# A gated block on one core: LoRA coefficients transposed two weight pieces later, and GpSimd's work cut into strips

## The chip, the cores and the metric

The kernel runs on one core of a Trainium2 chip. The core has five engines with queues of their own: TensorE (PE in the profile, with its weight loads as PEld), VectorE (DVE), ScalarE (ACT), GpSimd (POOL), and SyncE (SP), which here only starts transfers. Each works through its instructions in the order in which they are written and waits for others by semaphores. The metric is the device time of one execution in microseconds; the median of three executions stands for the kernel.

## What is computed

Two layers over 2048 tokens of width 2048 (the two batches of 1024 lie one after the other). The first multiplies the normalised and quantised tokens with a quantised context matrix of their batch. The second is a dense product with a weight matrix plus a mixture of eight LoRA experts of rank 16, of which a router picks two for each token.

```python
def fake_quant(x, s, z):
    return (jnp.clip(jnp.round(x / s + z), 0, 255) - z) * s

x = x + tanh(g_xattn[0]) * matmul(fake_quant(layernorm(x), s1, z1), fake_quant(ctx, s2, z2))

h = layernorm(x)
base = jnp.einsum('bsd,od->bso', h, base_W)
probs = softmax(jnp.einsum('bsd,ed->bse', h, router_W))
top_vals, top_idx = jax.lax.top_k(probs, 2)
w_dense = (one_hot(top_idx, 8) * (top_vals / top_vals.sum(-1, keepdims=True))[..., None]).sum(-2)
mid = jnp.einsum('bsd,edr->bser', h, lora_A) * w_dense[..., None]
x = x + tanh(g_ffn[0]) * (base + jnp.einsum('bser,erd->bsd', mid, lora_B) * 2.0)
```

## The kernel before, in words

**First stage (0 to some 300 us of the span).** Sixteen tiles of 128 tokens go through statistics and scale on VectorE (`x_stats`, `x_scale`), quantisation on ScalarE (`x_to_u8`), widening to bf16 on either (`x_widen`, tile `a_rows`), a transposition on TensorE (line 1361, tile `aT_psum`) and a copy back. They are multiplied with the context in 64 units of 16 matmuls (line 1374). VectorE empties each unit's bank into the tile of x (`evac`, line 1048). The order of all this is written out by hand in slot tables (`SCALE_SLOT`, `UNIT_SLOT`, `COLADD_SLOT` and others, 558 slots): each engine runs over the slots and does what its tables hold for a slot.

**GpSimd's part.** It has three kinds of work. `row_term` (line 677) adds a number per token to a whole tile of x, 128x2048, 16 times, and must be done before the tile's first `evac`. `add_col_term` (line 685) adds a row to a block of 128x512 after its `evac`, 64 times; the stores of x and the statistics of the second layer wait for it. `t_step` (line 694) subtracts two 128x1024 halves of the weights in f32, 32 times: these are the sums of weight blocks of a Strassen product, in eight jobs of four steps. Jobs 0 and 1 run by the slot tables in the first stage, jobs 2 to 7 in the second. Each step waits for the one before it by a semaphore, the first of a job for its load. A job's result is stored to `w_sums_scratch` by SyncE, and the load of job j from 4 on waits for the store of job j-2, in the same queue that loads the weights.

**Second stage.** The tokens go in four groups of 512. For the first group the plain product is taken: four blocks of 512 output columns (`plain_block`), each over eight weight pieces of 256 rows, 24 matmuls of 128x512 each, and a piece of LoRA B. `at_piece` counts the weight pieces of this group, 0 to 31, and every engine's program is laid out by it. A piece is loaded by SyncE into one of six buffers, its high part is made by ScalarE (`w_hi`, line 802) and its low part by VectorE (`w_lo`, line 1082), three pieces ahead of its product, and each product is three matmuls (lines 1389 to 1391). In f32 the low part is `w_stage` minus `w_hi`, both in SBUF.

While TensorE multiplies pieces 0 to 3, VectorE also works out the router's weights in eight parts (`router`, lines 1140 to 1172), each behind a `w_lo` in its order. The last part writes `mid_scaled`. TensorE transposes it into `col_psum` (`mid_transposes`, line 1447), ScalarE makes its high part (`mth`, line 881) and VectorE its low part (`mid_lo`, line 1182, semaphore `mtl_ready`). The LoRA products that end each block need both. In the kernel before, TensorE transposes right after the products of piece 4, ScalarE copies in its step for piece 5, VectorE in its step for piece 6, and TensorE waits for `mtl_ready` ahead of piece 7's products. The other three groups (the Strassen part, from about 502 us) have transposes of their own, in slot 4.

Of the kernel before, what the change touches and what calls it, by code (L numbers as in the profile page):

```python
# [25 lines left out]
ALU = mybir.AluOpType  # L26
# [107 lines left out]
SLOTS_G = 14  # L134
JOBS = 8
GROUPS = (2, 0, 1, 3)
FILL_AT = (8, 9, 10, 11, 13, 14, 16, 17)
# [129 lines left out]
def build(nc, x, ctx, wt, ar, lb, scal, x1s, wts, out):  # L267
    es = ExitStack()
    with es:
# [392 lines left out]
        def _(pool):  # L662
# [11 lines left out]
            def row_term(t):  # L674
                pool.wait_ge(row_ready, t + 1)
                tile = xg[(t // M) % 2][:, t % M, :]
                pool.tensor_scalar(tile, tile, crow[:, t:t + 1], 1.0, ALU.add, ALU.mult).then_inc(xr_ready, 1)

            def add_col_term(p):
# [3 lines left out]
                pool.wait_ge(bank_read, p + 1)  # L683
                blk = xg[(t // M) % 2][:, t % M, n * NW:(n + 1) * NW]
                pool.tensor_tensor(blk, blk, colb[n][:, :], ALU.add).then_inc(x1_ready, 1)

            def t_step(j, i):
# [5 lines left out]
                to, left, right = ((b11, b12, b11), (b12, b22, b12), (b22, b22, b11), (b21, b21, b22))[i]  # L693
                pool.tensor_tensor(to, left, right, ALU.subtract).then_inc(job_step, 1)  # L694

# [27 lines left out]
        def _(act):  # L723
# [143 lines left out]
            for i, (g, kind, s, pc) in enumerate(PIECES):  # L867
# [6 lines left out]
                if g == 0:  # L874
                    at_piece = WP * (s - 1) + pc
                    if at_piece == 2:
                        act.wait_ge(lg_ready, 1)
                        act.activation(ex[:, :, :], lg[:, :, :], ACT.Exp).then_inc(ex_ready, 1)
                    if at_piece == 5:
                        act.wait_ge(mt_ready, 1)  # L880
                        act.activation(mth[:, :], colp[:, :], ACT.Copy).then_inc(mth_ready, 1)
# [69 lines left out]
        def _(dve):  # L951
# [280 lines left out]
            for i, (g, kind, s, pc) in enumerate(PIECES):  # L1232
# [13 lines left out]
                if g == 0:  # L1246
                    at_piece = WP * (s - 1) + pc
                    if at_piece < 4:
                        router(chain, 0, 2 * at_piece)
                        router(chain, 0, 2 * at_piece + 1)  # L1250
                    if at_piece == 6:
                        mid_lo(0)
# [100 lines left out]
        def _(pe):  # L1353
# [144 lines left out]
            def plain_block(n):  # L1498
                for pp in range(WP):
# [7 lines left out]
                    else:  # L1507
                        if n == 0:
                            pe.wait_ge(mtl_ready, 1)
                        wait_lo(pe, i + 1)  # L1510
                        for m in range(M):
                            for kk in range(WK):
                                ins = plain_product(n, pp, m, kk)
                            if m == M - 1:
                                ins.then_inc(w_used, 1)
                            ins = three(bank(0, n + 1, m)[:, :], mth[:, tok(m)], mtl[:, tok(m)],
                                        wh[(i + 1) % HI][:, 0:NW], wl[(i + 1) % RAW][:, 0:NW], False, True)
                            ins.then_inc(acc_done, 1)
                    at_piece = WP * n + pp
                    if at_piece == 4:  # L1520
                        mid_transposes(0)
# [85 lines left out]
```

## Time and profile before

| | |
|---|---|
| median of 3 runs | 1071.0 us (1069.11 to 1071.47) |
| profiled execution | 1067.92 us, span 1066.2 us |
| TensorE busy | 1021.6 us, 96% of the span |
| VectorE busy | 788.1 us, 74% (252 us of the first 301) |
| ScalarE busy | 482.1 us, 45% |
| GpSimd busy | 208.3 us, 20%, all before 424 us |
| GpSimd by kind | 32 job steps 83.8 us, 64 column adds 91.1 us, 16 row terms 32.5 us |
| DMA | 249 GB/s over the span |

All times inside the kernel are counted in the profiled execution, from the start of its span. A duration of a DVE or POOL instruction in the trace includes the time for which it was held up after its start. Matmul durations are modelled and overlap; the spacing of their starts is what one costs. Where several instructions of a line follow one another, a row merges them and gives their count as x3.

### The profile page before, as it was taken

The numbers are of one execution on the slowest core, as the hardware profiler recorded it, in microseconds if no ns is written. First come the engines' busy times: TensorE is split into PE (matmuls) and PEld (weight loads), VectorE is DVE, ScalarE is ACT, GpSimd is POOL, SyncE is SP. The second block draws the span as 40 slices with busy tenths as digits, with TensorE's granted clock in tenths as the row PEclk, the third lists the DMA queues.
The fourth block names the chain that finished last, engine by engine and source line by source line (L and its number), as shares of the span: only waits on it lengthen the run. The fifth ranks groups of instructions, "written<-read, shape, count | busy, mean of one in ns | idle before, by whom it ended". The sixth has DMA issues, their size and how long they took to land.

```text
span 1066.2 us, 13135 instructions
## 1 busy us (share of the span) xinstructions
PE 1021.6 (96%) x5048; PEld 771.0 (72%) x5072; DVE 788.1 (74%) x1089; ACT 482.1 (45%) x503; POOL 208.3 (20%) x123
## 2 busy tenths in 40 slices
PE   2899999989997999999999999999999999999998
PEld 1444444444786888888887888898788889888887
DVE  7999897997579644457688678968867897855554
ACT  7864785340341223233444535644443555433432
POOL 2345554668233547000000000000000000000000
PEclk9999999989998999999999999999999999999999
DMA  8794599553696998553776876868687586568765
GB/s 341 298 407 173 217 359 392 220 171 127 222 362 267 356 321 327 206 173 105 217 299 193 281 274 195 269 184 311 189 276 276 180 277 188 195 203 295 251 199 179
DMA packets 85198, 265.89 MB, mean 249 GB/s; under 512 B 7312, under 2 KB 15504, under 8 KB 77456
## 3 DMA queue, kind: packets, MB, share of 16 engines
q1 hardware_dynamic: 67472, 231.50, 62.2%
q10 hardware_dynamic: 17664, 33.56, 8.5%
q8 instruction: 40, 0.66, 0.2%
q14 instruction: 22, 0.18, 0.1%
HBM read 214.70 MB, written 50.33 MB: 249 GB/s over the span
## 4 chain that ended last, share of the span: by engine, by line
PE 74%; DVE 16%; DMA 4%; ACT 3%; issue 3%; SPq 0%; ACTq 0%; DVEq 0%
PE acc L1374 16%; PE acc L1389 15%; PE acc L1391 15%; PE acc L1390 15%; DVE w_lo L1082 4%; PE aT_psum L1459 2%; DVE S_sum L1215 1%; PE aT_psum L1437 1%; PE aT_psum L1438 1%; DMA w_stage<-in_wt 1%; DVE S_lo L1223 1%; PE aT_psum L1361 1%; DVE c_acc L1193 1%; DMA w_stage<-w_sums_scratch 1%; ACT w_hi L802 1%
## 5 line engine op out<-in xcount | busy, mean ns | idle before, releaser
L1082 DVE TENSOR_TENSOR w_lo<-w_stage,w_hi 128x1024 fp32r<-128x1024 f32 x200 | 249.5, 1258 | 167.1 <-ACT w_hi L802 166.5
L802 ACT ACTIVATE w_hi<-w_stage 128x1024 fp32r<-128x1024 f32 x200 | 209.5, 1058 | 334.7 <-PE acc L1391 236.5
L1389 PE MATMUL acc<-w_hi,S_hi 128*128 128x512 f32 x384 | 151.4, 394 | 2.1 <-DVE w_lo L1082 1.7
L1391 PE MATMUL acc<-w_hi,S_lo 128*128 128x512 f32 x384 | 149.8, 390 | 0.0
L1390 PE MATMUL acc<-w_lo,S_hi 128*128 128x512 f32 x384 | 149.5, 389 | 0.0
L1389 PE MATMUL acc<-w_hi,A_hi 128*128 128x512 f32 x288 | 114.0, 396 | 0.3
L1374 PE MATMUL acc<-ctx_quant,aT_odd 128*128 128x512 bf16 x499 | 112.7, 383 | 0.9 <-issue 0.2
L1374 PE MATMUL acc<-ctx_quant,aT_even 128*128 128x512 bf16 x501 | 111.8, 381 | 1.2 <-ACT aT_even L760 0.6
L1391 PE MATMUL acc<-w_hi,A_lo 128*128 128x512 f32 x288 | 112.4, 390 | 0.0
L1390 PE MATMUL acc<-w_lo,A_hi 128*128 128x512 f32 x288 | 112.2, 390 | 0.0
L694 POOL TENSOR_TENSOR t_job<-t_job 128x1024 f32<-128x1024 f32 x32 | 83.8, 2621 | 82.7 <-DMA t_job<-in_wt 81.1
L1374 PEld LDWEIGHTS acc<-ctx_quant,aT_even 128*128 128x128 bf16 x512 | 49.9, 98 | 61.0 <-issue 1.8
L1374 PEld LDWEIGHTS acc<-ctx_quant,aT_odd 128*128 128x128 bf16 x512 | 50.2, 99 | 59.5 <-issue 2.5
L1193 DVE SCALAR_TENSOR_TENSOR c_acc<-acc,gates,c_acc 128x512 f32<-128x512 f32 x98 | 70.4, 746 | 24.0 <-PE acc L1391 23.6
L1389 PE MATMUL acc<-w_hi,hT_hi 128*128 128x512 f32 x224 | 88.0, 393 | 0.0
L1390 PE MATMUL acc<-w_lo,hT_hi 128*128 128x512 f32 x224 | 87.3, 390 | 0.0
L1391 PE MATMUL acc<-w_hi,hT_lo 128*128 128x512 f32 x224 | 87.3, 390 | 0.0
L1389 PEld LDWEIGHTS acc<-w_hi,S_hi 128*128 128x128 f32 x384 | 72.1, 188 | 17.6 <-DVE w_lo L1082 3.3
L1391 PEld LDWEIGHTS acc<-w_hi,S_lo 128*128 128x128 f32 x384 | 72.1, 188 | 15.2
L1390 PEld LDWEIGHTS acc<-w_lo,S_hi 128*128 128x128 f32 x384 | 72.2, 188 | 14.5
L752 ACT ACTIVATE ctx_u<-ctx_stage,scalars,constants 128x2048 uint16<-128x2048 f32 x32 | 66.3, 2087 | 25.6 <-DMA ctx_stage<-in_ctx 18.9
L1389 PEld LDWEIGHTS acc<-w_hi,A_hi 128*128 128x128 f32 x288 | 54.1, 188 | 11.8 <-DVE w_lo L1080 1.1
(182 smaller groups left out, 1607.9 us busy)
## 6 DMA issues: line engine op xcount, KB each, us to landing
w_stage<-in_wt SPq DMA_DIRECT2D x104, 512.0 KB, 4.7
w_stage<-w_sums_scratch SPq DMA_DIRECT2D x96, 512.0 KB, 4.3
ctx_stage<-in_ctx SPq DMA_DIRECT2D x32, 1024.0 KB, 7.8
t_job<-in_wt SPq DMA_DIRECT2D x8, 2048.0 KB, 10.5
w_sums_scratch<-t_job SPq DMA_DIRECT2D x8, 2048.0 KB, 13.3
c_acc<-x_scratch SPq DMA_DIRECT2D x32, 512.0 KB, 5.2
out<-c_acc ACTq DMA_DIRECT2D x64, 256.0 KB, 5.5
x_rows<-x_scratch SPq DMA_DIRECT2D x11, 1024.0 KB, 8.2
```

The source lines that it names most:

```text
L694: pool.tensor_tensor(to, left, right, ALU.subtract).then_inc(job_step, 1)
L752: act.activation(ctxu[:, c % NB, PK * p:PK * (p + 1), :], cst[q % CS][:, :, :], ACT.Identity, scale=inv2, bias=z2).then_inc(cu_ready, 1)
L802: ins = act.activation(wh[i % HI][:, :], raw[:, :], ACT.Copy)
L1082: ins = dve.tensor_tensor(low[:, :], raw[:, :], high[:, :].bitcast(F32), ALU.subtract)
L1193: dve.scalar_tensor_tensor(out=blk, in0=bank(g, s, part)[:, :], scalar=gate2, in1=blk, op0=ALU.mult, op1=ALU.add).then_inc(c_added, 1)
L1215: dve.tensor_tensor(half(dst, h), half(a, h), half(b, h), op).then_inc(combo_sum, 1)
L1223: dve.tensor_tensor(half(clo[name], h), half(src, h), half(chi[name], h).bitcast(F32), ALU.subtract)\
L1374: ins = pe.matmul(acc[p % M][:, :], aT[g % 2][:, k, m * P:(m + 1) * P], ctxq[:, c % NB, k, :], start=(k == 0), stop=(k == K - 1))
L1389: pe.matmul(out_, lh, rh, start=first, stop=False, skip_group_check=onto)
L1390: pe.matmul(out_, lh, rl, start=False, stop=False, skip_group_check=onto)
L1391: return pe.matmul(out_, ll, rh, start=False, stop=final, skip_group_check=onto)
L1459: ins = pe.transpose(tpb[done % 2][:, kk * P:(kk + 1) * P], rows_of(g, m)[:, (4 * f + kk) * P:(4 * f + kk + 1) * P], idf[:, :])
```

## The change

The transposes of `mid_scaled` for the first group move from behind piece 4 to behind piece 6 on TensorE, the ScalarE copy from step 5 to step 7, and VectorE's low part from step 6 to step 7. In the first block TensorE now does all products of piece 7 ahead of the wait for `mtl_ready`, and then the four LoRA products in a row. On GpSimd a row term becomes four instructions of 512 columns, a column add two of 256, and a job step four of 256; the semaphore rises with the last strip.

```diff
+STRIP = 256
...
             def row_term(t):
                 pool.wait_ge(row_ready, t + 1)
                 tile = xg[(t // M) % 2][:, t % M, :]
-                pool.tensor_scalar(tile, tile, crow[:, t:t + 1], 1.0, ALU.add, ALU.mult).then_inc(xr_ready, 1)
+                for a in range(0, D, NW):
+                    part = tile[:, a:a + NW]
+                    ins = pool.tensor_scalar(part, part, crow[:, t:t + 1], 1.0, ALU.add, ALU.mult)
+                ins.then_inc(xr_ready, 1)
...
-                blk = xg[(t // M) % 2][:, t % M, n * NW:(n + 1) * NW]
-                pool.tensor_tensor(blk, blk, colb[n][:, :], ALU.add).then_inc(x1_ready, 1)
+                for a in range(0, NW, STRIP):
+                    blk = xg[(t // M) % 2][:, t % M, n * NW + a:n * NW + a + STRIP]
+                    ins = pool.tensor_tensor(blk, blk, colb[n][:, a:a + STRIP], ALU.add)
+                ins.then_inc(x1_ready, 1)
...
-                pool.tensor_tensor(to, left, right, ALU.subtract).then_inc(job_step, 1)
+                for a in range(0, WK * NW, STRIP):
+                    part = slice(a, a + STRIP)
+                    ins = pool.tensor_tensor(to[:, part], left[:, part], right[:, part], ALU.subtract)
+                ins.then_inc(job_step, 1)
...
-                    if at_piece == 5:
+                    if at_piece == 7:
                         act.wait_ge(mt_ready, 1)
                         act.activation(mth[:, :], colp[:, :], ACT.Copy).then_inc(mth_ready, 1)
...
-                    if at_piece == 6:
+                    if at_piece == 7:
                         mid_lo(0)
...
                         if n == 0:
+                            for m in range(M):
+                                for kk in range(WK):
+                                    ins = plain_product(n, pp, m, kk)
+                            ins.then_inc(w_used, 1)
                             pe.wait_ge(mtl_ready, 1)
                         wait_lo(pe, i + 1)
                         for m in range(M):
-                            for kk in range(WK):
-                                ins = plain_product(n, pp, m, kk)
-                            if m == M - 1:
-                                ins.then_inc(w_used, 1)
+                            if n > 0:
+                                for kk in range(WK):
+                                    ins = plain_product(n, pp, m, kk)
+                                if m == M - 1:
+                                    ins.then_inc(w_used, 1)
                             ins = three(...)
                             ins.then_inc(acc_done, 1)
...
-                    if at_piece == 4:
+                    if at_piece == 6:
                         mid_transposes(0)
```

## Rows read from the trace of the kernel before

**Rows 1.** Who TensorE waited for: line and tile, releaser, us in total, times, longest.

```profile
PE aT_psum L1361 <- DVE a_rows L1003: 8.3, 4, 3.3
PE col_psum L1447 <- DVE mid_scaled L1172: 7.0, 1, 7.0
```

**Rows 2.** Chain that ended last, 300 to 345: start us, us, what.

```profile
317.42 3.45 DVE w_lo L1082
...
332.26 1.22 DVE w_lo L1082
...
335.37 1.12 PE col_psum L1447 x4
```

**Rows 3.** TensorE timeline, 335 to 339: start us, us, engine, line, instruction, shape, count.

```profile
335.37 1.12 PE L1447 MATMUL col_psum<-identity_f,mid_scaled 128*128 128x128 f32 x4 [6.98 <-DVE mid_scaled L1172]
336.14 0.78 PE L1389 MATMUL acc_even<-w_hi,hT_hi 128*128 128x512 f32 x1
...
338.41 0.39 PE L1391 MATMUL acc<-w_hi,hT_lo 128*128 128x512 f32 x1
338.64 0.40 PE L1389 MATMUL acc<-w_hi,hT_hi 128*128 128x512 f32 x1
```

**Rows 4.** Stretches: window, PE, PEld, DVE, ACT, POOL busy; clock; DMA share; GB/s.

```profile
210.00:240.00 30.00, 26.39 (x133) 12.93 (x134) 28.04 (x44) 12.13 (x8) 20.50 (x13) 0.89 0.45 153
330.00:340.00 10.00, 4.63 (x16) 3.88 (x17) 9.52 (x23) 2.08 (x3) 0.49 (x1) 0.66 0.59 247
343.00:440.00 97.00, 97.00 (x462) 80.92 (x461) 46.13 (x60) 26.39 (x37) 43.97 (x16) 1.00 0.91 330
```

**Rows 5.** TensorE timeline of the first stage: transposes that waited.

```profile
108.44 1.07 PE L1361 MATMUL aT_psum<-identity_bf,a_rows 128*128 128x128 bf16 x16 [1.85 <-DVE a_rows L1003]
137.13 1.07 PE L1361 MATMUL aT_psum<-identity_bf,a_rows 128*128 128x128 bf16 x16 [0.80 <-DVE a_rows L1003]
220.21 1.89 PE L1361 MATMUL aT_psum<-identity_bf,a_rows 128*128 128x128 bf16 x16 [3.34 <-DVE a_rows L1003]
```

**Rows 6.** VectorE timeline ahead of the wait that ends at 220.

```profile
207.40 2.14 DVE L993 SCALAR_TENSOR_TENSOR newton<-x_rstd,x_var_eps 128x1 f32<-128x1 f32 x1
...
209.76 2.20 DVE L995 SCALAR_TENSOR_TENSOR quant_scale_bias<-x_rstd,constants,newton 128x1 f32<-128x1 f32 x1
...
215.68 2.27 DVE L996 SCALAR_TENSOR_TENSOR quant_scale_bias<-x_mean_var,quant_scale_bias,scalars 128x1 f32<-128x1 f32 x1
```

**Rows 7.** Durations by line, all instructions: count, ns shortest/median/longest.

```profile
L993 DVE SCALAR_TENSOR_TENSOR newton<-x_rstd,x_var_eps x16: 219/744/2136, 12.1 to 232.7; 128x1 f32<-128x1 f32 x16
L1048 DVE SCALAR_TENSOR_TENSOR x_group_even<-acc,constants,x_group_even x32: 737/745/751, 36.9 to 222.3; 128x512 f32<-128x512 f32 x32
```

**Rows 8.** The same durations for GpSimd's three kinds of work.

```profile
L694 POOL TENSOR_TENSOR t_job<-t_job x32: 2342/2400/3405, 207.2 to 420.6; 128x1024 f32<-128x1024 f32 x32
L685 POOL TENSOR_TENSOR x_group_even<-x_group_even,col_term x32: 1262/1271/3182, 42.4 to 223.2; 128x512 f32<-128x512 f32 x32
L677 POOL TENSOR_SCALAR x_group_odd<-x_group_odd,row_terms x8: 1972/1975/1979, 84.5 to 244.3; 128x2048 f32<-128x2048 f32 x8
```

**Rows 9.** Five column adds in a row on GpSimd, and VectorE beside them.

```profile
86.49 6.17 POOL L685 TENSOR_TENSOR x_group_even<-x_group_even,col_term 128x512 f32<-128x512 f32 x5
...
90.45 1.00 DVE L995 SCALAR_TENSOR_TENSOR quant_scale_bias<-x_rstd,constants,newton 128x1 f32<-128x1 f32 x1
```

**Rows 10.** ScalarE timeline: three waits, on GpSimd, on TensorE, and on a load.

```profile
268.86 1.07 ACT L795 ACTIVATE ar_hi_lo<-w_stage 128x272 fp32r<-128x272 f32 x3 [22.32 <-POOL x_group_odd L685]
...
336.53 0.60 ACT L881 ACTIVATE midT_hi<-col_psum 128x512 fp32r<-128x512 f32 x1 [7.41 <-PE col_psum L1447]
...
403.07 1.06 ACT L802 ACTIVATE w_hi<-w_stage 128x1024 fp32r<-128x1024 f32 x1 [8.17 <-DMA w_stage<-in_wt]
```

**Rows 11.** TensorE timeline: first LoRA A product, first matmul on the piece of 403.

```profile
278.61 0.37 PE L1437 MATMUL acc<-ar_hi_lo,hT_hi 128*128 128x272 f32 x1
...
414.26 0.47 PE L1389 MATMUL acc_even<-w_hi,hT_hi 128*128 128x512 f32 x1
```

## Prediction

> **What bounds the kernel now.** I read first who TensorE waited for, since it is busy 96% of the span. Behind the start-up fill there are two things: widened x tiles made by VectorE, 8.3 us in four waits, and the router's result for the LoRA part, 7.0 us in one wait [rows 1]. Everything else is TensorE's own work, so a change gains only what it takes out of these waits.
>
> Then I read what VectorE did ahead of them. In the chain of waits before 335 us stands a `w_lo` of 3.45 us, although another takes 1.22 in the same chain [rows 2]. The surplus, 2.2 us, is nearly one job step of GpSimd (2.34 to 2.40 us [rows 8]). Before 220 us one-column operations take 2.14, 2.20 and 2.27 us [rows 6]; their shortest is 0.22 [rows 7]. The stretched ones all read two tiles of SBUF (or write f32 or bf16 at the fast rate); `evac`, which reads a PSUM bank and one tile, never leaves 0.74 to 0.75 [rows 7]. So a VectorE operation with two SBUF inputs that meets a GpSimd instruction waits until that instruction ends.
>
> The Trainium skill, "SBUF — State Buffer", Who interferes with whom, has the rule: the shared port is an exclusive lock, and whichever engine starts first holds it for its whole instruction. The trace agrees with it here (2.2 us of surplus beside steps of 2.34).
>
> **The wait at 328 us: its price.** TensorE sits idle 6.98 us [rows 3]. After it the granted clock is low: 0.66 on average from 330 to 340 [rows 4], that is 1.2 GHz for a while. From 336.14 to 338.64 lie six matmuls [rows 3]: 2.50 us. The last of them, 338.41 to 338.64, costs 0.23 again; six of these are 1.38. That is 1.1 us, and the four transposes in front, 0.77 us from start to start [rows 3], lose half, 0.4. Together 6.98 + 0.16 + 1.1 + 0.4 = 8.6 us.
>
> **The move, part by part.** *Removed*: the wait in front of the transposes. Piece 4 ends at 328.4, and TensorE goes on with pieces 5 and 6. A piece is 24 matmuls at 0.227, 5.45 us, so the transposes come at about 339.2, and the result has been there since 335.4 [rows 2]. *What is late next*: the low part of piece 6. It starts at 332.26 and takes 1.22 [rows 2], so it is there at 333.5, and TensorE asks for it at 333.8. This is close, but the strips (below) pull it forward by over 10 us, because small router operations behind job steps are held up like that `w_lo`. *Added*: ScalarE's copy (0.60 us [rows 10]) and `mid_lo` now lie behind one more weight conversion each. ScalarE's step 7 begins when piece 6 is used, 339.2: conversion 1.06, copy 0.60, to about 340.9; VectorE converts its piece until 342.5 and is done with `mid_lo` at 343.2. TensorE meanwhile has transposes (0.4) and piece 7's 24 products until 345.1, which is why they are placed ahead of the wait: 2 us of cover, and without the reordering the wait would be some 3.5 us. *Queued behind*: nothing on TensorE; on ScalarE the next conversions, which have three pieces (16 us) of lead. The reordering delivers the first block's banks 2 us before its end and 0.7 apart instead of 2 apart. VectorE empties each in 0.75 us (as `evac` [rows 7]); TensorE asks for the second one 0.7 us into the next block, some 1.2 us after it is free. Price 0. SyncE gets `w_used` of piece 7 earlier.
>
> So this part gives 8.6 us. The strips alone would also remove this wait: nine operations from 310 to 330 wait 2.2 us less 0.4, which brings the router forward some 15 us. The gain is counted once.
>
> **The strips: what they cost GpSimd.** From 512 columns at 1.26 to 1024 at 2.34 us [rows 8] a column costs 2.1 ns and an instruction 0.18. A strip of 256 is then 0.72 us. A job step becomes 4 x 0.72 = 2.9 (+0.55), a column add 1.44 (+0.18), a row term, with the same 0.18 taken as fixed, 4 x 0.63 = 2.5 (+0.54). Sum 32 x 0.55 + 64 x 0.18 + 16 x 0.54 = 37.8 us, so GpSimd is busy about 246 us instead of 208. Bounds for the extra per strip: 0, when strips overlap (five adds take 6.17 us in a row, 1.23 each and not 1.27 [rows 9]), and 0.18 from the fit.
>
> **What they give VectorE.** A held-up operation waits at most 0.72 us, 0.36 on average, instead of up to 2.4. In the chain to the wait at 220 the rows show 1.9 + 2.0 + 2.05 us of hold-up [rows 6, 7], and three smaller ones with some 2 us. Six of 0.36 are 2.2, six of 0.72 are 4.3: the chain shortens by 3.7 to 5.8 us, and the wait is 3.34 [rows 5]. It goes, and so does its low clock: 0.89 over 210 to 240 [rows 4] is 0.11 x 30 x 2 = 6.6 us at 1.2 GHz, of which TensorE worked some 5 (1.89 for 16 transposes instead of 1.07 [rows 5]), a loss of about 2.5. The waits of 1.85 and 0.80 [rows 5] have chains of the same kind; there TensorE comes 0.5 and 2.4 us earlier than before, and the held-up operations (1.0 to 1.7 us each) give 3 to 4 back. Together 3.34 + 2.5 + 1.85 + 0.80 + some 0.5 in one more = 9.0 us at most. The first of the four waits (in the fill) has no held-up operation in front of it and stays. I take 7.5 of 9.0, because the chains shorten by only 1 to 2 us more than they must.
>
> **Who waits for GpSimd's longer chain.** At the end of the first stage ScalarE stood 22.3 us in a store that waits for a column add, until 268.86 [rows 10], and the LoRA A pieces queue behind it. From 242 to 268 GpSimd does eight adds, a row term and four job steps: 8 x 0.18 + 0.54 + 4 x 0.55 = 4.2 us more. Their conversion ends at 269.9 [rows 10], VectorE's low part takes up to 2 us more, and the first product starts at 278.6 [rows 11]: 6.8 us of lead, so it is covered; without cover it would cost 4.2. In the second stage `store_job` is in SyncE's queue ahead of weight loads, and each job ends 2.2 us later. The tightest load I find was converted at 403.07, 8.2 us after ScalarE asked [rows 10], and was first used at 414.26 [rows 11], so about 9 us of lead behind both conversions. Price 0; if uncovered, 2 us.
>
> **Sum.** 8.6 + 7.5 = 16.1 us. Against the profiled execution, 1067.9, that is 1052; its median is 3.1 us higher, which no row explains, so against the median 1071.0 I predict **1055 us**. The range of the forecast alone is 1051 to 1059.
>
> **Rivals.** *(A) Only half of the first stage comes back.* TensorE, early by 3 us, meets loads or hold-ups of 0.72 each time: 8.6 + 4 gives 1058.5. For it: VectorE is busy 28 of 30 us before the wait [rows 4]. Against: no wait of TensorE for a context tile stands among its waits. *(B) Strips in a row do not let VectorE in.* Job steps were separated by a semaphore; strips are not. Then a hold-up is the whole former instruction and its 0.55 us: the surplus, some 43 us in the first stage, grows by a quarter, TensorE's waits there by 3 us, and the router comes at 340 for the transposes at 339. 8.6 - 3 - 0.7 = 5 gives 1066. Against: among five adds back to back a one-column operation took 1.00 us, not the rest of the 6.17 [rows 9].
>
> "GPSIMD Engine Reference", 2.1 Instruction dispatch, in the Trainium skill says that each of the eight cores starts its next instruction as soon as its own share is done. By that rule strips without a wait between them could overlap and never let go of the port, which is (B). Whether they do no row here can show.
>
> *(C) Transfers take the wait's place.* DMA was 0.91 busy from 343 to 440 [rows 4] and idle during the wait. Squeezing the same bytes into 8.6 us less makes it about 0.95; if loads then come late, they give up to 7 us back: 1062. *(D) Slower: GpSimd becomes the bound.* If a strip costs f more than 0.72, GpSimd's queue from 242 to 268 grows by 23 x f on top of 4.2. Past the 6.8 us of cover, from f = 0.11, TensorE waits; past 16 + 2.6 us, f = 0.8, the kernel is slower than before; at f = 1.0, 23 - 2.6 - 16 = 4 us slower here alone, 1075. Against: the fit's whole fixed share is 0.18. *(E) The move does nothing by itself*, since the strips already bring the router forward: this is so by the sum above, and changes no time.
>
> **Chances.** Forecast 0.66, A 0.12, C 0.07, B 0.08, both gains eaten up by new waits (within 0.2%) 0.03, D 0.04. The range of 1049 to 1063 leaves out B, D, the even case and a little of the forecast. A measurement of this kernel can tell about 0.2%, 2.1 us, from no change. Faster 0.92, same 0.04, slower 0.04.
>
> **What would show it.** Right: no wait of TensorE at `col_psum` for the first group; `router_rank` never above 1 us; no one-column operation above 1 us; the wait at 220 gone and the granted clock 1.00 in both stretches; GpSimd busy 235 to 250 us; ScalarE's wait for the last column add not followed by an idle TensorE. Wrong: hold-ups of 2 us or more beside strips (B), or TensorE waiting for `ar_hi_lo` around 270 or `w_hi` around 400 (D, C).

## The result, and the profile after

The changed kernel takes 1054.66 us in the median of six runs (1050.25 to 1056.62), against 1070.03 for the kernel before on the same chip: a ratio of 0.986 [0.984, 0.988], 15.4 us less. The profiled execution took 1053.84 us against 1067.92, 14.1 us less. Predicted were 1055 us and a gain of 16.1 us, so the time came out as predicted. Its reasons did so only in part.

The page of the kernel after, busy time of each engine:

```profile
PE 1018.3 (97%) x5048; PEld 769.2 (73%) x5072; DVE 761.2 (72%) x1089; ACT 482.2 (46%) x503; POOL 270.8 (26%) x331
```

VectorE is busy 27 us less with the same work, GpSimd 62 us more. Who TensorE waited for, behind the start-up fill, in the kernel after (columns as in [rows 1]):

```profile
PE aT_psum L1370 <- DVE a_rows L1012: 1.7, 1, 1.7
PE acc L1398 <- DVE w_lo L1091: 1.6, 1, 1.6
...
PE col_psum L1456 <- DVE mid_scaled L1181: 1.1, 1, 1.1
...
PE acc L1383 <- issue: 0.8, 1, 0.8
```

Of the four waits for widened x tiles [rows 1] the one in the fill is left. The 7.0 us at `col_psum` are gone; the 1.1 us that stand there now belong to a later group. Three stretches, with the columns of [rows 4], in the kernel after; the third is the work that lay from 343 to 440 before, about 16 us earlier now:

```profile
210.00:240.00 30.00, 29.02 (x169) 14.53 (x170) 26.40 (x51) 12.12 (x9) 26.96 (x41) 1.00 0.56 194
315.00:325.00 10.00, 10.00 (x46) 8.29 (x45) 9.72 (x17) 3.18 (x4) 9.84 (x12) 1.00 0.93 359
327.00:424.00 97.00, 97.00 (x464) 80.91 (x463) 47.87 (x63) 26.63 (x38) 61.97 (x71) 1.00 0.92 341
```

The granted clock is 1.00 (2.4 GHz) where it was 0.89, and in the stretch around the transposes' old place. The transfers are 0.92 busy over this work, as against 0.91 before, and TensorE waits for none of them.

**Where the time came out.** Three edges cut the span: the first matmul on a weight piece of the first group, the first one of the later groups, and the last. They stand in the rows of the `w_hi` line (count, ns shortest/median/longest, first to last start). Before:

```profile
L1389 PE MATMUL acc<-w_hi,A_hi x288: 387/389/481, 502.3 to 1061.2; 128*128 128x512 f32 x144
L1389 PE MATMUL acc_even<-w_hi,hT_hi x32: 389/389/775, 301.0 to 448.6; 128*128 128x512 f32 x32
```

After:

```profile
L1398 PE MATMUL acc<-w_hi,A_hi x288: 389/389/481, 486.5 to 1047.1; 128*128 128x512 f32 x144
L1398 PE MATMUL acc_even<-w_hi,hT_hi x32: 389/389/476, 293.7 to 432.8; 128*128 128x512 f32 x32
```

The first stage is 7.3 us shorter (301.0 to 293.7; predicted 7.5), the first group 8.5 us (201.3 to 192.8; predicted 8.6), and the later groups 1.7 us longer (558.9 to 560.6; predicted 0). That is 14.1 us. Both large terms have their predicted size. Which edit earned each is a question for the runs.

### The profile page after: what moved, and what is told of

Same layout as the page of the kernel before. It is cut to its first block, busy times and chain, and to the rows that moved or that the text cites. A ratio compares the mean times of both kernels' runs of the same rounds, so it can differ in the third digit from the quotient of the medians.

```text
span 1052.1 us, 13343 instructions
## 1 busy us (share of the span) xinstructions
PE 1018.3 (97%) x5048; PEld 769.2 (73%) x5072; DVE 761.2 (72%) x1089; ACT 482.2 (46%) x503; POOL 270.8 (26%) x331
## 4 chain that ended last, share of the span: by engine, by line
PE 76%; DVE 11%; DMA 6%; ACT 4%; issue 2%; SPq 0%; ACTq 0%; DVEq 0%
PE acc L1398 17%; PE acc L1400 16%; PE acc L1399 16%; PE acc L1383 15%; DMA ctx_stage<-in_ctx 3%; DVE w_lo L1091 3%; PE aT_psum L1468 2%; ACT ctx_u L761 2%; DVE S_sum L1224 1%; PE aT_psum L1446 1%; PE aT_psum L1447 1%; DVE S_lo L1232 1%; DMA w_stage<-w_sums_scratch 1%; PE aT_psum L1370 1%; DVE c_acc L1202 1%
## 5 line engine op out<-in xcount | busy, mean ns | idle before, releaser
L702 POOL TENSOR_TENSOR t_job<-t_job 128x256 f32<-128x256 f32 x128 | 107.7, 872 | 56.4 <-DMA t_job<-in_wt 54.8
L690 POOL TENSOR_TENSOR x_group_even<-x_group_even,col_term 128x256 f32<-128x256 f32 x64 | 59.3, 961 | 37.5 <-DVE col_term L1049 30.5
```

What stands on the lines that cost most here:

```text
L690: ins = pool.tensor_tensor(blk, blk, colb[n][:, a:a + STRIP], ALU.add)
L702: ins = pool.tensor_tensor(to[:, part], left[:, part], right[:, part], ALU.subtract)
```

## What the experiments had to tell apart

The prediction gave 8.6 us to the move and 7.5 us to the strips, and said that the strips alone would earn both. Its rival E added that beside the strips the move does nothing; that the move might do nothing even without them was not foreseen. Within the strips it was open which of GpSimd's three kinds of work held VectorE up where. Nine kernels take the change apart, one overdoes it, one is the change again, and one goes further. Each was compared with the kernel before on its own chip.

### The move alone

```diff
# after, with GpSimd's three kinds of work whole again
-                for a in range(0, D, NW):
-                    part = tile[:, a:a + NW]
-                    ins = pool.tensor_scalar(part, part, crow[:, t:t + 1], 1.0, ALU.add, ALU.mult)
-                ins.then_inc(xr_ready, 1)
+                pool.tensor_scalar(tile, tile, crow[:, t:t + 1], 1.0, ALU.add, ALU.mult).then_inc(xr_ready, 1)
...
# add_col_term and t_step likewise
```

> Only the transposes of the first group are moved; GpSimd's instructions are whole, as before. My theory: the wait of 6.98 us at piece 4 and its low clock go (8.6 us), and nothing is gained in the first stage, since its waits come from hold-ups by whole GpSimd instructions: about 1061.5, ratio 0.992. TensorE's other waits stay as before: 3.3 us at about 220 with the granted clock low there, 1.85 and 0.80 at 108 and 137. Piece 6's low part is ready only 0.3 us ahead of use, so a wait of up to 1 us may stand there. Rival (the move itself pays for everything): about 1055. Rival (the router's result is still late at piece 6): 1063 or more, with a wait at col_psum.

Measured: 1068.15 us, ratio 0.9991 [0.9975, 1.0007]: no change, where 1061.5 was expected. The wait at `col_psum` is gone, and another stands in its place. TensorE's waits in this kernel:

```profile
PE aT_psum L1362 <- DVE a_rows L1004: 6.0, 4, 1.9
PE acc_even L1390 <- DVE midT_lo L1183: 4.8, 1, 4.8
...
PE aT_psum L1460 <- DVE x_rows L1206: 1.8, 1, 1.8
```

VectorE's timeline there (start us, us):

```profile
336.15 2.46 DVE L968 BATCH_NORM_STATS2 bn_chunks_group<-x_rows 128x6 f32<-128x512 f32 x4
...
339.62 2.46 DVE L968 BATCH_NORM_STATS2 bn_chunks_group<-x_rows 128x6 f32<-128x512 f32 x4
...
344.45 1.35 DVE L1206 TENSOR_SCALAR x_rows<-x_rows,mean_var,rstd 128x2048 f32<-128x2048 f32 x1
345.71 3.36 DVE L1083 TENSOR_TENSOR w_lo<-w_stage,w_hi 128x1024 fp32r<-128x1024 f32 x1
349.00 0.68 DVE L1183 TENSOR_TENSOR midT_lo<-col_psum,midT_hi 128x512 fp32r<-128x512 f32 x1
```

and GpSimd's:

```profile
344.66 11.58 POOL L695 TENSOR_TENSOR t_job<-t_job 128x1024 f32<-128x1024 f32 x4 [13.62 <-DMA t_job<-in_wt]
```

I had `mid_lo` done at 343.2; it is done at 349.7. Two things took the 2 us of cover. The router is as late as before, so what follows it in VectorE's order, two rounds of statistics of 2.46 us and a normalisation of 1.35, is late too and stands ahead of the low part. And since TensorE no longer waits, SyncE comes to the load of job 4 ten us earlier (333.2 instead of 343.3); its first step begins at 344.66, in front of a `w_lo`, which takes 3.36 us instead of 1.22. TensorE waits 4.8 us for `midT_lo`. (The 1.8 us for `x_rows` stand in a later group, beyond 700 us.) Behind the wait the granted clock falls (columns as in [rows 4]):

```profile
350.00:355.00 5.00, 5.00 (x16) 3.93 (x16) 2.88 (x4) 0.57 (x1) 4.84 (x3) 0.66 0.09 35
```

The twelve LoRA matmuls there take 4.2 us, where twelve at 0.227 are 2.7. So the new wait costs 4.8 + 1.5 = 6.3 us. Another 0.5 us goes at 333.3 for the low part of piece 6, which the prediction had called close. The first group takes 200.3 us, 1.0 less than before.

### Job 4 in strips beside the move

```diff
# move_only, with
+                width = STRIP if j in (4,) else WK * NW
+                for a in range(0, WK * NW, width):
```

> The move alone, with only the four steps of job 4 in strips; jobs 2 and 3 whole. In the kernel with the move alone, SyncE came to job 4's load 10 us earlier, its steps began at 344.7 and held up the w_lo ahead of mid_lo by 2.1 us; TensorE waited 4.8 us. Theory: that hold-up shrinks to 0.7 us or less, the rest of the wait is VectorE's backlog behind the late router (two row statistics of 2.5 us, a normalisation) and stays: a wait of 2.8 to 3.6 us for midT_lo, time 1.5 us below that of the move alone, ratio 0.997. Rival (job 4 makes all of the wait): no wait, 5 us less, ratio 0.994.

Measured: 1064.74 us, ratio 0.9959 [0.9943, 0.9976]. TensorE's wait in this kernel:

```profile
PE acc_even L1394 <- DVE midT_lo L1187: 3.2, 1, 3.2
```

VectorE there:

```profile
345.71 1.75 DVE L1087 TENSOR_TENSOR w_lo<-w_stage,w_hi 128x1024 fp32r<-128x1024 f32 x1
347.38 0.68 DVE L1187 TENSOR_TENSOR midT_lo<-col_psum,midT_hi 128x512 fp32r<-128x512 f32 x1
```

The same `w_lo` at the same moment falls from 3.36 to 1.75 us, and the wait from 4.8 to 3.2, both by 1.6. So a third of that wait was job 4's. The rest is the backlog behind the late router, by the order of VectorE's instructions; no run takes it away by itself. The first group takes 197.6 us instead of 200.3. The whole profiled execution (span 1066.5) is not shorter than that of the move alone: it was the slowest of this kernel's twelve, and its first stage and later groups were longer.

### The strips without the move

```diff
# after, with the move taken back
-                    if at_piece == 7:
+                    if at_piece == 5:
                         act.wait_ge(mt_ready, 1)
...
-                    if at_piece == 7:
+                    if at_piece == 6:
                         mid_lo(0)
...
-                    if at_piece == 6:
+                    if at_piece == 4:
                         mid_transposes(0)
# and the first block's products of piece 7 in their old order
```

> Only the strips; transposes stay behind piece 4. My theory: the router's result comes at about 319, 2 us or more before piece 4 ends, so there is no wait at col_psum and the time is that of the full change, 1054.7 within 2 us (ratio 0.986): the move gives nothing by itself. Rival (both parts are needed): the wait at col_psum is shorter but there, 2 to 4 us, and the time is 1057 to 1060. In this order TensorE then waits for mtl_ready ahead of piece 7; copy and low part are long done by then, so no wait.

Measured: 1055.61 us, ratio 0.9871 [0.9852, 0.9891], the whole gain. The profiled execution's span is 1052.0 us, against 1052.1 with the move. VectorE in this kernel:

```profile
314.08 1.67 DVE L1091 TENSOR_TENSOR w_lo<-w_stage,w_hi 128x1024 fp32r<-128x1024 f32 x1
...
316.43 3.01 DVE L1181 TENSOR_TENSOR mid_scaled<-mid,expert_weights 128x128 f32<-128x128 f32 x4
```

`mid_scaled` is written by 319.4, and TensorE gets to its transposes at 321.7: they find their data there. Before, it was written at 335.4 [rows 2]. The router comes 16 us earlier, but 6.5 of these are the shorter first stage (294.5 instead of 301.0). Counted from the start of the group it is written after 24.9 us instead of 34.4: 9.5 us earlier, not the 15 that the prediction took from shorter hold-ups. Part of the difference is `mid_scaled` itself, whose four operations take 3.01 us here and 1.27 before, when GpSimd had already finished. TensorE needed 7.0, so 2.3 us are left over. Rival E holds: the move earns nothing here.

### Jobs 2 and 3 alone in strips

```diff
# before, with
+                width = STRIP if j in (2, 3) else WK * NW
+                for a in range(0, WK * NW, width):
```

> The kernel before with one edit: the steps of jobs 2 and 3 (the eight that run beside the router) in strips of 256; transposes stay behind piece 4, everything else whole. Theory now: the wait at col_psum is made by these eight steps alone. It goes, with its low clock, and nothing else changes: 8.6 us less, ratio 0.992, about 1061 against 1069. TensorE's loss in the first block 0.3 us or less. Rival (taking the wait away lets job 4 start early and hold up VectorE, as in the kernel with the move alone, where TensorE then waited 4.8 us for midT_lo): about 1066. I expect no such wait, since mid_lo is then done 8 us before job 4's steps start.

Measured: 1060.93 us, ratio 0.9918 [0.9897, 0.9939]. The first group takes 193.0 us instead of 201.3, so all of that gain comes from eight of the 32 job steps. The wait of 4.8 us for `midT_lo` does not appear, as expected. The stretch around the router in this kernel (columns as in [rows 4]):

```profile
315.00:340.00 25.00, 25.00 (x113) 20.67 (x113) 21.67 (x36) 6.55 (x9) 19.13 (x23) 1.00 1.00 374
```

TensorE is busy throughout at a clock of 1.00; in the kernel before it sat idle for 7 us and worked at 0.66 behind that [rows 3, 4].

### Row and column strips, and job strips, each beside the move

```diff
# strips_x_only: after, with t_step whole
+                pool.tensor_tensor(to, left, right, ALU.subtract).then_inc(job_step, 1)
# strips_jobs_only: after, with row_term and add_col_term whole
```

> The move, with row terms and column adds in strips, but job steps whole (128x1024, 2.4 us). My theory: the waits of 1.85 and 0.80 us and one of 0.5 go, the one at about 220 stays for the most part, because the instructions ahead of it were held up by job steps: 8.6 + 3.2 us of gain, about 1059. Rival (column adds do the harm there too): nearer 1055. The one-column operations before 220 should still show up to 2.2 us, elsewhere at most 0.75.

> The move, with job steps in strips, but row terms (2.0 us) and column adds (1.26 us) whole. My theory: the wait at about 220 and its low clock go (5.9 us), the waits of 1.85, 0.80 and 0.5 us stay: 8.6 + 5.9 us of gain, about 1055.5 to 1057. Together with the kernel that cuts only row terms and column adds the gains of the first stage should add up to that of the full change (9 us in all).

Measured: 1060.02 us, ratio 0.9916 [0.9892, 0.994], and 1056.18 us, ratio 0.9896 [0.9866, 0.9925]. The first one's time is near the expected one, but it is earned elsewhere. Edges and waits of the kernel with row and column strips alone:

```profile
L1395 PE MATMUL acc<-w_hi,A_hi x288: 387/389/481, 493.1 to 1054.7; 128*128 128x512 f32 x144
L1395 PE MATMUL acc_even<-w_hi,hT_hi x32: 389/389/498, 292.4 to 439.4; 128*128 128x512 f32 x32
```

```profile
PE acc_even L1395 <- DVE midT_lo L1188: 4.8, 1, 4.8
```

Edges of the one with job strips alone:

```profile
L1393 PE MATMUL acc<-w_hi,A_hi x288: 389/389/481, 489.4 to 1048.8; 128*128 128x512 f32 x144
L1393 PE MATMUL acc_even<-w_hi,hT_hi x32: 389/389/476, 296.6 to 435.7; 128*128 128x512 f32 x32
```

With whole job steps the first stage still ends at 292.4 (four executions with whole row and column steps and whole jobs 0 and 1 gave 298.0 to 301.0, mean 299.9: 7.5 us), and the first group keeps its 200.7 us, with the 4.8 us wait of the move alone. With job strips it is the other way: 3.3 us in the first stage, and 192.8 us for the first group. The two gains belong to two kinds of work: the first stage to row and column strips, the first group to job strips.

The two gains of the first stage, 7.5 and 3.3 us, do not add up to that of all strips (299.9 to 293.3 in the mean of four executions, 6.6 us). The traces show why: either kind of strip removes the wait at 220 by itself. In the kernel before, two steps of job 0 begin just ahead of the first of the one-column operations of [rows 6]:

```profile
207.18 4.78 POOL L694 TENSOR_TENSOR t_job<-t_job 128x1024 f32<-128x1024 f32 x2 [4.32 <-DMA t_job<-in_wt]
```

The operations at 207.40 and 209.76 last until these steps end. In the kernel with row and column strips and whole job steps, VectorE (two rows) and GpSimd:

```profile
204.57 0.22 DVE L999 SCALAR_TENSOR_TENSOR newton<-x_rstd,x_var_eps 128x1 f32<-128x1 f32 x1
...
208.02 2.23 DVE L999 SCALAR_TENSOR_TENSOR newton<-x_rstd,x_var_eps 128x1 f32<-128x1 f32 x1
```

```profile
205.46 4.78 POOL L700 TENSOR_TENSOR t_job<-t_job 128x1024 f32<-128x1024 f32 x2 [3.01 <-DMA t_job<-in_wt]
```

VectorE comes 2.8 us earlier and is through with the first set before job 0 begins. Only one operation of the chain, the one at 208.02, meets a step, the tile is widened from 211.5 instead of 217.9, and TensorE does not wait for it. With job strips alone TensorE does not wait at 220 either, but its waits of 1.85 and 0.80 us at 108 and 137 stay:

```profile
PE aT_psum L1365 <- DVE a_rows L1007: 3.7, 3, 1.9
```

So job steps did stretch the chain to 220, as the prediction read it. What the prediction did not see is that cutting the other two kinds of work moves VectorE out of their way.

### Jobs 0 and 1 whole again

```diff
# after, with
+                width = STRIP if j in (2, 3, 4, 5, 6, 7) else WK * NW
+                for a in range(0, WK * NW, width):
```

> The changed kernel, but with the steps of jobs 0 and 1, which run in the first stage, whole again. With row terms and column adds alone in strips the first stage lost least (14.6 us beyond TensorE's own work, against 16.0 in the changed kernel, where a wait of 0.8 us at 224 came from GpSimd's longer queue: a store in ScalarE's queue waited for a column add, and a copy of aT behind it). Theory: first stage as in that kernel, first block as in the changed one: 1 to 1.5 us faster than the changed kernel, about 1053.3 on the scale where before is 1070 (ratio 0.9845). Rival (steps of 2.4 us hold up the chain to the tile transposes at 220 again, as in the kernel before): 2 to 5 us slower than the changed kernel, ratio 0.988 to 0.990.

Measured: 1053.62 us, ratio 0.986 [0.9838, 0.9882], no different from the full change. The rival did not happen, though two one-column operations were held up for 2.0 and 2.4 us from 204.3 on: TensorE waited 0.43 us for the tile. The experiment looks at a small wait that the change brings in. TensorE in the kernel after:

```profile
224.29 1.89 PE L1383 MATMUL acc<-ctx_quant,aT_odd 128*128 128x512 bf16 x7 [0.82 <-issue]
```

ScalarE:

```profile
222.32 1.88 ACT L769 ACTIVATE aT_odd<-aT_psum 128x2048 bf16<-128x2048 bf16 x1 [4.73 <-POOL x_group_even L690]
```

GpSimd:

```profile
215.48 4.97 POOL L702 TENSOR_TENSOR t_job<-t_job 128x256 f32<-128x256 f32 x7
220.41 1.41 POOL L690 TENSOR_TENSOR x_group_even<-x_group_even,col_term 128x256 f32<-128x256 f32 x2
```

ScalarE's copy for TensorE stands behind a store that waits for a column add, and this stands in GpSimd's queue behind job strips. It is rival D at a size of 0.8 to 1.3 us. With jobs 0 and 1 whole it is not there. The first stage then ends at 291.9, 292.4 and 292.0 (this kernel, the one with row and column strips alone, and the last one below), against 294.5, 293.7, 292.6 and 292.4 in the four executions with all strips of 256: 1.2 us in the mean, the size of that wait, but less than the 3 us by which this edge differs among executions of the same code. So its worth in time is not shown.

### Strips of 64 and 128 columns

```diff
-STRIP = 256
+STRIP = 64
...
-                for a in range(0, D, NW):
-                    part = tile[:, a:a + NW]
+                for a in range(0, D, 2 * STRIP):
+                    part = tile[:, a:a + 2 * STRIP]
```

> The changed kernel with strips a quarter as long: 64 columns for column adds and job steps, 128 for row terms. By the fit (0.18 us fixed, 2.1 ns a column) a job step is 16 x 0.32 = 5.0 us, a column add 8 x 0.32 = 2.5, a row term 16 x 0.3 = 4.7: GpSimd needs 40 + 161 + 75 = 276 us for its part of a first stage of 300 us, hold-ups not counted. Theory (price of strips, my rival D): GpSimd becomes the bound of the first stage, VectorE and ScalarE wait for column adds, TensorE for them: 10 to 30 us slower than the kernel before. Rival (strips overlap in GpSimd and cost only their columns): GpSimd 210 to 230 us, time as the changed kernel, 1055.

Measured: 1150.54 us, ratio 1.0744 [1.0712, 1.0776]: some 80 us slower, not 10 to 30. Rival D is real, and it sets in with the size of the strip. The page of this kernel, its busy times and GpSimd's slices:

```profile
PE 1041.9 (91%) x5072; PEld 777.6 (68%) x5072; DVE 742.9 (65%) x1089; ACT 481.5 (42%) x503; POOL 443.2 (39%) x1291
...
POOL 3969997699993699990000000000000000000000
```

GpSimd's timeline and the waits:

```profile
251.92 9.05 POOL L702 TENSOR_TENSOR t_job<-t_job 128x64 f32<-128x64 f32 x32
```

```profile
ACT ar_hi_lo L804 <- POOL x_group_odd L690: 41.6, 1, 41.6
...
PE acc L1383 <- issue: 20.7, 2, 15.5
PE acc L1410 <- DVE x_group_odd L1057: 17.2, 1, 17.2
```

A strip of 64 costs 0.28 us where nothing is in the way (expected 0.32), so it was not the price of the instruction that I got wrong. GpSimd is full through most of the first 500 us, all that waits for its adds is late (TensorE 15.5 and 17.2 us in single waits), and the first group begins at 372.2 instead of 293.7. The first group is 18.6 us longer too (211.4 instead of 192.8), with 8.3 us in one wait for `hT_A`, a tile of transposed tokens that ScalarE copies. The expectation left hold-ups out: by its fit GpSimd needs 160 + 161 + 75 = 396 us in the whole kernel, and it is busy 443. In the prediction, rival D counted extra work only from 242 to 268, where the first product on LoRA A waits, and not all the stores and statistics before it.

### GpSimd almost silent

```diff
-                for a in range(0, D, NW):
-                    part = tile[:, a:a + NW]
+                for a in range(0, 1):
+                    part = tile[:, a:a + 1]
# and so in add_col_term and t_step
```

> The changed kernel with nearly no work on GpSimd: each of its steps touches one column only, with the same waits and signals, so the row terms, column adds and weight sums are left out of the result. It prices what hold-ups and GpSimd's own time still cost. Theory: VectorE's hold-ups in the first stage fall from 25 us to 2 or less; TensorE enters the first block at 291 to 292 instead of 293.7, and nothing changes behind it: 2 to 3 us faster than the changed kernel, ratio 0.983 to 0.984. Rival (hold-ups are still a large cost): 5 us or more, ratio 0.981 or less.

Measured: 1052.51 us, ratio 0.9861 [0.9823, 0.9899]; the change itself, run beside it:

> The changed kernel once more, beside the others on one chip. Both theories: ratio 0.986. The profile is a second look at the same code: it tells how much TensorE's losses differ from one execution to the next. I expect the end of the first stage at 293.7 within 1 us and 192.8 us for the first group's four blocks, and the spread of 6 us between executions to lie in the three later groups, where transfers land late in some executions.

1054.77 us, ratio 0.9867 [0.9843, 0.989]. Its profile has the first stage at 292.6, the first group at 194.2 us (192.8 was expected; TensorE waits once in it, 1.1 us for `hT_A`) and the later groups at 561.4. So the same code differs by 1 us or so in each part, and not in the later groups alone.

With GpSimd nearly taken away the median is 2.3 us lower than with all its work in strips, the ratio only 0.0006: nothing that the intervals can tell. TensorE enters the first block at 291.3, as expected. So what GpSimd cost TensorE, some 15 us, is as good as gone at 256 columns, and smaller strips have nothing more to win.

### TensorE waits ahead of piece 7's products

```diff
                         if n == 0:
-                            for m in range(M):
-                                for kk in range(WK):
-                                    ins = plain_product(n, pp, m, kk)
-                            ins.then_inc(w_used, 1)
                             pe.wait_ge(mtl_ready, 1)
# the products are taken behind the wait, as in the kernel before
```

> The changed kernel, but in the first block TensorE waits for midT_lo ahead of piece 7's products, as the kernel before does. By the trace of the changed kernel midT_lo is done at 335.6 and those products start at 332.2: a wait of 3.4 us, ratio 0.989. Rival (the order of the products does not matter): ratio 0.986, no wait.

Measured: 1058.51 us, ratio 0.9915 [0.9885, 0.9946], with this wait of TensorE:

```profile
PE acc_even L1398 <- DVE w_lo L1091: 2.7, 1, 2.7
```

The row names `w_lo`, but the low part that these products need had long been written. The matmul starts at 333.8, when `midT_lo` has just ended (333.7): what TensorE waits for is `mtl_ready`. The first group takes 195.7 us, against 192.8 and 194.2 in the two profiles of the full change. The prediction had 3.5 for the wait. The median is 3.7 us above that of the full change on the same chip, and the two intervals just touch; the profiled execution (span 1052.7) doesn't show that, as its later groups were 1 us shorter than in the kernel after and its first stage 1.3. So the move most likely has a cost in this place, and its own reordering pays for it: taken together the two come to nothing.

### The same reordering in the later groups

The `w_lo` wait of 1.6 us in the kernel after is of this kind too. TensorE in it:

```profile
540.41 0.66 PE L1456 MATMUL col_psum<-identity_f,mid_scaled 128*128 128x128 f32 x4 [1.10 <-DVE mid_scaled L1181]
...
548.12 0.47 PE L1398 MATMUL acc<-w_hi,S_hi 128*128 128x512 f32 x1 [1.58 <-DVE w_lo L1091]
```

VectorE:

```profile
546.20 1.22 DVE L1091 TENSOR_TENSOR w_lo<-w_stage,w_hi 128x1024 fp32r<-128x1024 f32 x1
547.33 0.68 DVE L1191 TENSOR_TENSOR midT_lo<-col_psum,midT_hi 128x512 fp32r<-128x512 f32 x1
```

The matmul that starts at 548.12 starts when `midT_lo` ends (548.0), not when `w_lo` does (547.4). In slot 4 of a later group twelve products of the last piece need no LoRA term and can go ahead of that wait:

```diff
# jobs01_whole, with
+                        first = s == 4
+                        if first:
+                            for t in range(2):
+                                for kk in range(WK):
+                                    ins = product(t, kk)
+                            ins.then_inc(w_used, 1)
                         if LORA[r]:
...
                         for t in range(2):
-                            for kk in range(WK):
-                                ins = product(t, kk)
-                            if t == 1 and LORA[r]:
-                                ins.then_inc(w_used, 1)
+                            if not first:
+                                for kk in range(WK):
+                                    ins = product(t, kk)
+                                if t == 1 and LORA[r]:
+                                    ins.then_inc(w_used, 1)
```

> Jobs 0 and 1 whole, everything else as changed, and one edit in the later groups: in their slot 4 TensorE takes the 12 products of the last piece ahead of its wait for midT_lo, as the change does for the first group. In the changed kernel TensorE stands there 1.75, 0.6 and 0.56 us in the three groups, and where the weights of that slot land late it also stands 1.1 us ahead of the transposes. Theory: products of 2.7 us cover the first three waits; 2 to 4 us faster than the changed kernel, about 1050 to 1052 where before is 1070, ratio 0.982. Rival (VectorE's lateness there only moves on to the next pieces): within 1 us of the kernel with jobs 0 and 1 whole, ratio 0.986.

Measured: 1048.57 us, ratio 0.9812 [0.9786, 0.9838]; the full change on the same chip was 1054.77. Edges and the remaining wait in slot 4:

```profile
L1399 PE MATMUL acc<-w_hi,A_hi x288: 387/389/481, 487.1 to 1043.4; 128*128 128x512 f32 x144
L1399 PE MATMUL acc_even<-w_hi,hT_hi x32: 389/389/478, 292.0 to 433.4; 128*128 128x512 f32 x32
```

```profile
PE col_psum L1457 <- DVE mid_scaled L1182: 0.5, 1, 0.5
```

No `w_lo` wait is left; the same kernel without the reordering (jobs 0 and 1 whole) had 3.2 us of them in two waits. The later groups take 556.3 us from the first row to the last start, against 558.9 to 563.3 in all the other kernels. The first group is longer here, 195.1 us, with TensorE waits of 1.0 us for `hT_A` and 0.6 us for `c_acc`. This is the fastest kernel of the study. The next of those that compute everything is the one with jobs 0 and 1 whole, 1053.62 on another chip: 5 us. The full change on the same chip is 6.2 us slower, more than the 2 to 4 expected, but it differs in jobs 0 and 1 as well. So the reordering most likely brings some 5 us; the two kernels that differ in it alone were not run side by side.

## Why the prediction was right, and where not

**The number.** Right, and the two terms of the sum have their sizes: 7.3 us in the first stage for 7.5, and 8.5 us in the first group for 8.6. The one term that I had at zero and that moved is the later groups, 1.7 us longer. Kernels with the same orders of TensorE there differ from 558.9 to 563.3 us, so that is no cost of the change that the runs can show.

**The move (8.6 us credited to it).** This step failed. By itself the move is worth nothing (0.9991 [0.9975, 1.0007]), and the strips alone are worth everything (0.9871 [0.9852, 0.9891]). "VectorE ... is done with `mid_lo` at 343.2" was 349.7, because I costed VectorE's steps behind the router at their old times, although the router was as late as ever, and because I moved TensorE earlier without moving what its progress triggers: SyncE's load of job 4, and with it job steps into the very stretch. The price of the wait, 8.6 us, was right, as the kernel with jobs 2 and 3 in strips gave 8.3, though its term of 0.16 rests on no row. What the move did not foresee is that a new wait costs clock as well: 4.8 us idle and 1.5 us of slow matmuls. That the strips alone would remove it was in the text too, and carried the total. Rival E, which the sum already implied, held, and the move earned nothing without the strips either.

**What strips cost.** The price of a strip was right: 0.72 us fitted, and 0.715 as the shortest in the kernel after (shortest/median/longest):

```profile
L702 POOL TENSOR_TENSOR t_job<-t_job x128: 715/737/1797, 205.1 to 409.6; 128x256 f32<-128x256 f32 x128
```

The sum was not: GpSimd is busy 270.8 us, not 246, and outside the 235 to 250 that were named as a sign. 256 strips at 0.715 and 64 at 0.685 are 227 us; the other 43 us I put down to hold-ups by VectorE. In the kernel before the same reckoning, 32 x 2.342 + 64 x 1.262 + 16 x 1.972 = 187, leaves 20 us. I had let the hold-ups of GpSimd stand as they were. Each strip is one more start at which it can find VectorE busy; that this is the reason was not tested. The change moved hold-up from the engine that matters to the one that had room.

**What strips give.** The mechanism was right, and the whole prediction lives on it. Router operations of 64 columns take 0.66 to 0.78 us beside strips, `router_rank` never more than 0.98, and an operation of 128x1 at most 0.76. The Trainium skill, "SBUF — State Buffer", Who interferes with whom, has the port held for a whole instruction; 0.755 us at the longest beside strips of 0.715 agrees. VectorE in the kernel after:

```profile
L1002 DVE SCALAR_TENSOR_TENSOR newton<-x_rstd,x_var_eps x16: 219/514/755, 12.1 to 226.8; 128x1 f32<-128x1 f32 x16
```

It was 2136 ns [rows 7]. Two sizes failed. The router gained 9.5 us from shorter hold-ups and not 15. And in the first stage the gains were added up wait by wait, as if one did not shift the next: row and column strips alone give 7.5 us, job strips alone 3.3, all of them together 6.6 to 7.3, because either kind removes the wait at 220. The 7.5 for the stage was itself a choice below a sum of 9.0, so that it came out so near is partly luck.

**The rivals.** A (half of the first stage) did not happen. B (strips do not let VectorE in) is refuted by the row just shown, by 0.66 us for `router_rank_eq` between strips in a row, and by the kernel with GpSimd silent, which is 2.3 us faster at most. The Trainium skill, "GPSIMD Engine Reference", 2.1 Instruction dispatch, has each of the cores start its next instruction as soon as its own share is done; whatever the overlap, it did not keep VectorE out here. C (transfers) did not happen: the DMA share over the same work is 0.92, below the 0.95 that C reckoned with, and TensorE waits for no load. D is there as 0.8 to 1.3 us at 224, and at 64 columns as 80 us; its direction and its place in GpSimd's queue were right, its size was far too small, because the cover was weighed at one wait out of many. Its factor is wrong too: the eight adds, the row term and the four job steps are 36 strips, of which 23 are additional, so a price of f more on every strip adds 36 x f and uses up the cover from f = 0.07.

**Still open.** What sets the spread of 3 us in the first stage (298.0 to 301.0) and of 4 us in the later groups among executions whose code there is the same, and with it what the wait at 224 is worth. Single profiles can't settle it.

## What to carry to other kernels

When the engine with slack and the engine without share a resource that is held for a whole instruction, look at the length of the instructions of the one with slack: here each additional instruction cost 0.17 us (four strips of 0.715 for one step of 2.342), and the other's small operations fell from 2.1 to 2.3 us to 0.76 at most, until, at 64 columns, its own queue became late. Gains taken wait by wait need not add up: two halves of a change can each remove the same wait. When a wait is removed by moving its consumer, redo the order of every engine behind it at the new times, transfers included, since an earlier TensorE starts loads earlier and these bring their own work into the gap. Run each half of a change alone before you credit it: here one half did all of it. A wait's row can name the wrong one of several semaphores, and asking which one it was led to the reordering behind the best kernel.

## What was not expected of the hardware

Strips in a row follow each other without a gap in the trace (ten column strips took 6.88 us, 0.69 each, less than the 0.715 of one alone), and VectorE still gets in between them, though GpSimd waits for no semaphore there: a one-column operation took 0.74 us beside those ten. Its hold-up is bounded by one strip, not by the row of strips. By the reckoning above the hold-up goes both ways, 20 us on GpSimd with long instructions and 43 us with short ones, while VectorE's busy time fell by 27 us.
